# Masked many-head cross-attention: scores by query for the maxima, and a second set by key for the exponentials

## The chip, the cores and the metric

One core of one Trainium2 chip runs the whole program in one launch. The metric is the device time in microseconds (us). The kernel before took 776.32 us (median of three runs, 772.29 to 776.37). The engines are PE (TensorE: matmuls and transposes, with PEld for its weight loads), DVE (VectorE), ACT (ScalarE), POOL (GpSimd) and SP (SyncE, which here issues the DMAs). Each engine works through its own list of instructions in order; semaphores tie the lists together.

## The reference, cut to what matters

A decoder of two layers works on x (16 sequences, 128 tokens, 256 channels). Each of six sublayers normalises x and adds its result: a one-head causal attention, a cross-attention with 16 heads and a boolean mask, a block-sparse feed-forward layer, a 16-head attention, a 16-head windowed attention with another mask, and a mixture of experts. The change is in the second:

```python
qh = (q @ Wq.T + bq).reshape(B, Sq, 16, 16)          # q: normalised x; k, v: ctx
kh = (k @ Wk.T + bk).reshape(B, Sk, 16, 16)
vh = (v @ Wv.T + bv).reshape(B, Sk, 16, 16)
scores = jnp.einsum('bqhd,bkhd->bhqk', qh, kh) / np.sqrt(16)
scores = jnp.where(attention_mask[:, None, :, :], -1e7, scores)
probs = jax.nn.softmax(scores, axis=-1)
out = jnp.einsum('bhqk,bkhd->bqhd', probs, vh)
```

For these inputs no position is masked, but the kernel does not know that and masks by the data.

## The kernel before, in words

The 16 sequences are worked in eight pairs of 256 tokens. A running number U counts pairs through the stages: U 0 to 7 is the one-head attention (stage 0), 8 to 15 the masked many-head stage (stage 1), 16 to 23 the feed-forward layer (stage 2), 24 to 31 the unmasked 16-head attention (stage 3), 32 to 39 the windowed one (stage 4); the experts follow. A loop over U calls `half(U, 0)` and `half(U, 1)` on every engine, one half for each sequence of the pair, and the order in which `half` and its `part0` to `part3` call their steps is the order of the engine's list, written by hand. Steps of pairs U-2 to U+2 lie in one half.

PSUM has eight banks of 128 x 512 numbers in three rings: `pj` (three banks, for projections and transposes), `sc` (four banks, for scores) and `ov` (one bank). A bank's `filled` semaphore counts what PE has put into it, and `drained` what DVE or ACT has taken out; PE waits for `drained` before it writes a bank again. The four heads of a bank make one "group" n, so a half has four groups, one in each `sc` bank.

Stage 1 before. `scores` puts queries on partitions and keys along the free axis. Two of a half's four groups get the mask by a matmul ahead of the scores (`preload`, L462), the two others by a DVE addition (`add_mask`, L1096). DVE takes row maxima (`row_maxima`, L1103), ACT the exponentials, four instructions of 128x128 a group with the maximum as bias (`row_exps`, L1651). The probabilities then have queries on partitions, and the product with the values needs keys there: PE transposes each group (`turn_probs`, L546), and DVE or ACT copies the result out (`copy_probs`, L1110). `probs_times_values` (L558) and `turn_out` (L567) follow, and `norm_heads` (L1133, L1137) divides by the sums.

Stages 3 and 4 do without the transposes. `by_query` (L485) computes scores only for the maxima (`maxima`, L1125). `turn_maxima` (L494) transposes the small table of maxima, ACT copies it out (L1627, mxT), and SP's `shift` (L2102) moves it by DMA into unused rows of the query tile qM, where it works as one more channel against a row of constants in the key tile kM. `by_key` (L514) then computes scores with keys on partitions and the maximum already subtracted, and ACT's `exps` (L1642) takes one 128x512 exponential a group straight from PSUM. `by_query` for a half is issued one half ahead: `following(U, j)` names the half whose maxima are taken while `by_key` of (U, j) is still to come. Both score sets go through the same four `sc` banks in turn.

The blank rows that SP writes to the experts' table (`blank_rows`) lie between the loads of the context in stage 1.

Of the kernel before, what the change touches and what calls it, by code (L numbers as in the profile page):

```python
# [24 lines left out]
P = 128  # L25
F32 = mybir.dt.float32
BF16 = mybir.dt.bfloat16
# [30 lines left out]
for _name, _n in (("bq0", C), ("bk0", C), ("b1", FF), ("bq1", 2 * C), ("bk1", 2 * C), ("gq", C), ("gk", C),  # L58
                  ("gv", C), ("go", C), ("mine", 2), ("unit", 2), ("quarter", 2), ("sixteenth", 2), ("place", B),
                  ("lane", 1)):  # L60
    VEC[_name] = (sum(n for _, n in VEC.values()), _n)
# [10 lines left out]
def program(nc, x, ctxT, ctx, tokq, tokk, mask, ident, causal, causalT, vec, rows, lnb, before, blank,  # L72
# [3 lines left out]
    with stack:  # L76
# [20 lines left out]
        bq = [sb(f"bq{i}", [P, (C, 2 * C)[i]]) for i in range(2)]  # L97
# [18 lines left out]
        def R(name):  # L116
# [23 lines left out]
        kraw = sb("kraw", [P, C, T])  # L140
# [32 lines left out]
        pT = [hT[1][:].rearrange("p a b -> p (a b)")[:, r * 4 * S:(r + 1) * 4 * S].rearrange("p (a s) -> p a s", a=4)  # L173
              for r in range(4)]
        mxg = [mx[0][:, r * 4:(r + 1) * 4] for r in range(4)]
# [68 lines left out]
        def sems(names):  # L244
# [11 lines left out]
        mx_done, ri_done, kM_done, masked_done, s_causT = sems("mx_done ri_done kM_done masked_done s_causT")  # L256
# [10 lines left out]
        spots_done, first_done, one_done, slot_done = sems("spots_done first_done one_done slot_done")  # L267
        den_done, dene_done, deni_done, share_done, comb_done = sems(
            "den_done dene_done deni_done share_done comb_done")
        cnt_done, step_done, many_done, upto_done, reach_done, behind_done, who_done, base_done, row_done, tab_done = sems(  # L270
            "cnt_done step_done many_done upto_done reach_done behind_done who_done base_done row_done tab_done")
# [10 lines left out]
        ACT_TURNS = {1: (2, 6)}  # L282
        DVE_MAXED = {4: (3, 7), 5: (3, 7), 6: ()}
# [23 lines left out]
        def overtaken(U, j):  # L307

            return stage(U) == 1 and (U % PAIRS, j) != (PAIRS - 1, 1)

        def shifted(U):

            return stage(U) in (3, 4)
# [69 lines left out]
        def _(pe):  # L383
# [112 lines left out]
            def by_key(U, j):  # L496

                f, p = U // PAIRS, U % PAIRS
                masks = {3: None, 4: mbT1}[f]
# [8 lines left out]
                pe.wait_ge(s_shift[j], 32 * (att(U) - PAIRS + 1))  # L508
# [10 lines left out]
            def scores(U, j):  # L519

                f, p = U // PAIRS, U % PAIRS
                if j == 0:
                    pe.wait_ge(*emptied("q", U))
                    pe.wait_ge(kM_done, att(U) + 1)
                sides = []
                for n in range(4 * j, 4 * j + 4):
                    b, k = begin("sc", "s", U, n)
                    pe.wait_ge(drained[b], k - 1)
                    added = n not in DVE_MASKED[f]
                    if added:  # L530
                        preload(b, mb0, p, j)
                    sides.append((b, slice(32 * (n % 4), 32 * (n % 4) + 32), added))
                for c in range(C):
                    for b, strip, added in sides:
                        last = mm(bank[b][:, c * T:(c + 1) * T], qT[U % 2][strip, c, j * S:(j + 1) * S],  # L535
                                  kM[U % 2][strip, c, :, j * S:(j + 1) * S], start=not added, stop=True,
                                  skip_group_check=True)
                        if c == C - 1:
                            last.then_inc(filled[b], 1)

            def turn_probs(U, n):
                b, k = begin("pj", "pT", U, n)
# [272 lines left out]
            def half(U, j):  # L815
# [4 lines left out]
                elif f == 1:  # L820
                    scores(U, j)
# [1448 lines left out]
```

## Time and profile before

| what | value |
|---|---|
| median of three runs | 776.32 us |
| the profiled execution | 779.23 us, span 777.4 us |
| PE busy | 742.5 us (96%) |
| DVE busy | 481.2 us (62%) |
| ACT busy | 389.0 us (50%) |
| POOL busy | 297.3 us (38%) |
| mean granted TensorE clock | 0.987 of full |

The profiled execution is one run; its span goes from the first to the last instruction, and its own time is 1.8 us longer. Busy shares are means over stages with different limits, so what a change in one stage is worth has to be read from that stage's stretch: here about 64 to 205 us.

### The profile page before, as it was taken

Reading aid. Unit: us, or ns where it says so; the run is one execution under the profiler, and the core shown is the slowest. Engines: PE = TensorE matmul, PEld = TensorE weight load, DVE = VectorE, ACT = ScalarE, POOL = GpSimd, SP = SyncE. Lnnn points to the kernel's source line nnn. Section 1 sums busy time; section 2 is a strip of 40 time slices with the busy share of each in tenths; the row PEclk is TensorE's granted clock in tenths of the full one; section 3 lists DMA queues with packets and bytes.
Section 4 is the critical chain, followed back from the end, with each engine's and each line's share of the span. In section 5 each row is a group of like instructions: output and inputs, shape, how many; then the busy total and the mean of one; then the engine's idle time right before and its main releaser. Section 6 shows DMA issues by size and latency. Waiting matters only on the chain.

```text
span 777.4 us, 19012 instructions
## 1 busy us (share of the span) xinstructions
PE 742.5 (96%) x7189; PEld 608.0 (78%) x7189; DVE 481.2 (62%) x1388; ACT 389.0 (50%) x951; POOL 297.3 (38%) x397
## 2 busy tenths in 40 slices
PE   8999999999999999999999999999999899899996
PEld 7887777776788888888888887777867667688885
DVE  4686787887654445356555566787856458554435
ACT  3445677777533233436666544444534266266630
POOL 2323333434224213211212255565656435545540
PEclk9999999999999999999999999999989899999999
DMA  8997244300256642101000021000000101245428
GB/s 310 402 220 145 76 109 117 78 15 2 62 139 165 166 128 70 56 2 30 4 3 3 4 90 51 16 16 16 16 30 16 36 31 41 90 138 155 145 87 320
DMA packets 67962, 69.92 MB, mean 90 GB/s; under 512 B 22721, under 2 KB 58561, under 8 KB 66849
## 3 DMA queue, kind: packets, MB, share of 16 engines
q1 hardware_dynamic: 64464, 59.37, 26.5%
q0 software_dynamic: 3408, 9.34, 3.5%
q8 instruction: 59, 0.97, 0.5%
q14 instruction: 31, 0.25, 0.1%
HBM read 39.03 MB, written 29.40 MB: 88 GB/s over the span
## 4 chain that ended last, share of the span: by engine, by line
PE 77%; DVE 10%; ACT 4%; issue 3%; POOL 2%; DMA 2%; SPq 1%; another core or an unknown queue 1%; DVEq 0%; POOLq 0%
PE pj L403 12%; PE pj L396 8%; PE sc L609 7%; PE ov L622 7%; PE ov L558 6%; PE sc L485 4%; PE sc L514 4%; PE pj L390 4%; PE ov L812 4%; PE sc L462 4%; PE sc L804 3%; DVE mx L1103 3%; PE pj L546 2%; PE sc L535 2%; PE pj L567 2%
## 5 line engine op out<-in xcount | busy, mean ns | idle before, releaser
L1642 ACT ACTIVATE pr<-sc 128x512 f32<-128x512 f32 x128 | 66.1, 606 | 72.9 <-PE sc L514 65.6
L1125 DVE TENSOR_REDUCE mx<-sc 128x4 f32<-128x512 f32 x120 | 74.5, 683 | 23.7 <-PE sc L485 21.5
L1651 ACT ACTIVATE pr<-sc,mx 128x128 f32<-128x128 f32 x256 | 72.9, 379 | 31.4 <-DVE mx L1103 30.3
L1883 POOL TENSOR_SCALAR ve<-mv 128x2 f32<-128x2 f32 x40 | 13.3, 333 | 180.6 <-DVE mv L1038 180.2
L609 PE MATMUL sc<-xnT,W 128*128 128x256 f32 x256 | 61.0, 382 | 0.8 <-DVE mx L1125 0.8
L1700 ACT ACTIVATE hT<-sc,vecs 128x256 f32<-128x256 f32 x64 | 30.1, 475 | 62.6 <-PE sc L609 62.6
L622 PE MATMUL ov<-W,hT 128*128 128x256 f32 x256 | 60.1, 379 | 0.0
L1627 ACT ACTIVATE oT<-ov 128x512 f32<-128x512 f32 x48 | 28.9, 602 | 53.9 <-PE ov L558 48.4
L622 PEld LDWEIGHTS ov<-W,hT 128*128 128x128 f32 x256 | 48.5, 190 | 6.7
L1961 POOL DMA_INDIRECT routed_y<-pr,mask x39 | 37.3, 955 | 41.5 <-DVE mask L1379 34.9
L609 PEld LDWEIGHTS sc<-xnT,W 128*128 128x128 f32 x256 | 47.3, 190 | 7.0 <-DVE mx L1125 1.0
L1103 DVE TENSOR_REDUCE mx<-sc 128x4 f32<-128x512 f32 x64 | 42.8, 684 | 13.8 <-PE sc L535 13.8
L1627 ACT ACTIVATE xnT<-pj 128x512 f32<-128x512 f32 (+1 forms) x79 | 38.7, 490 | 18.7 <-PE pj L390 11.3
L1913 POOL TENSOR_TENSOR hT<-hT,rws 128x512 f32<-128x512 f32 x16 | 20.4, 1274 | 63.1 <-DVE hT L1241 63.1
L804 PEld LDWEIGHTS sc<-xnT,cT 128*128 128x128 f32 x312 | 40.5, 191 | 2.5 <-issue 0.7
L546 PE MATMUL pj<-idn,pr 128*128 128x128 f32 x256 | 39.9, 282 | 2.6 <-ACT pr L1651 1.0
L514 PEld LDWEIGHTS sc<-qM,kM 32*128 32x128 f32 x1024 | 32.6, 192 | 12.5 <-issue 12.1
L804 PE MATMUL sc<-xnT,cT 128*128 128x128 f32 x312 | 41.3, 275 | 0.0
L558 PE MATMUL ov<-pr,va 128*32 128x128 f32 x1024 | 38.0, 276 | 3.1 <-issue 2.4
L485 PEld LDWEIGHTS sc<-kM,qM 32*128 32x128 f32 x1024 | 31.5, 186 | 11.0 <-issue 10.0
L546 PEld LDWEIGHTS pj<-idn,pr 128*128 128x128 f32 x256 | 27.6, 141 | 15.2 <-issue 9.5
L1133 DVE RECIPROCAL rin<-pj 128x16 f32<-128x16 f32 x48 | 12.1, 253 | 43.9 <-PE pj L567 36.3
(259 smaller groups left out, 1794.5 us busy)
## 6 DMA issues: line engine op xcount, KB each, us to landing
sorted_x<-more_xT SPq DMA_DIRECT2D x15, 1152.0 KB, 7.9
kM<-sorted_x SPq DMA_DIRECT2D x39, 129.0 KB
cT<-in_ctxT SPq DMA_DIRECT2D x16, 256.0 KB, 3.6
pr<-kept_at SPq DMA_DIRECT2D x32, 128.0 KB, 3.2
W<-in_w SPq DMA_DIRECT2D x2, 1024.0 KB, 13.5
cT<-in_ctx SPq DMA_DIRECT2D x8, 256.0 KB, 3.8
oT<-kept_at SPq DMA_DIRECT2D x16, 128.0 KB, 3.2
hd<-kept_at SPq DMA_DIRECT2D x16, 128.0 KB, 3.3
```

The lines of the kernel that those rows point to most:

```text
L403: last = mm(bank[b][:, j * n:(j + 1) * n], still[:, c, j * S:(j + 1) * S], w[:, c, col:col + n], start=c == 0, stop=c == C - 1)
L514: last = mm(bank[b][:, o:o + S], kM[U % 2][strip, c, i, s], qM[U % 2][strip, c, i, s], start=not added, stop=True, skip_group_check=True)
L546: last = tr(bank[b][:, i * S:(i + 1) * S], pr[n % 4][:, i, :], idn[:])
L558: last = mm(bank[b][32 * i:32 * i + 32, g * S:(g + 1) * S], va[U % 2][:, j, 4 * g + i, :], probs[g][:, i, :], start=True, stop=True, skip_ ...
L609: last = mm(bank[b][:, 0:T], W1[:, d, c * P:(c + 1) * P], xnT[U % 3][:, d, :], start=d == 0, stop=d == C - 1)
L622: last = mm(bank[b][:, j * D:(j + 1) * D], hT[U % 2][:, d, j * S:(j + 1) * S], W2[:, d, :], start=d == 0, stop=d == FF - 1)
L804: last = mm(bank[b][:, i * P:(i + 1) * P], tile_gu[t % 2][:, c, i * EI:(i + 1) * EI], xtT[t % 3][:, c * P:(c + 1) * P], start=c == 0, stop ...
L1103: v.tensor_reduce(mxg[n % 4], four(b), AX.X, ALU.max, negate=True).then_inc(mx_done, 1)
L1125: last = v.tensor_reduce(dst, bank[b][:, :].rearrange("p (c i s) -> p c i s", c=C, i=2), AX.X, ALU.max, negate=True)
L1627: a(dst, src, ACT.Copy, scale=scale).then_inc(drained[b], 1)
L1642: a(pr[n % 4][:], four(b), ACT.Exp).then_inc(drained[b], 1)
L1651: last = a(pr[n % 4][:, i, :], bank[b][:, i * S:(i + 1) * S], ACT.Exp, bias=mxg[n % 4][:, i:i + 1])
```

## The change

Stage 1 takes the form of stages 3 and 4. `scores`, `turn_probs` and their copies go. `by_query` masks all four groups of a half by `preload` with mb0. `by_key` masks nothing: ACT and DVE do it behind it, each for two groups of a half. For the groups 2 and 3, `add_mask` takes the minimum of a score and `hidden` (0 where the key is seen, -1e30 where not); a score less its maximum is never above 0. For the groups 0 and 1, ACT takes Relu of the negated score into SBUF and the exponential in place there, and DVE's `clip` takes the minimum with `seen` (1 or 0). `seen` and `hidden` come from a transposed copy of the mask (`maskT`, 256 KB, a new DMA) and lie in half of the tile that held the copied probabilities; `count_hidden` (four matmuls in all) finds queries that see no key, and `note_seen` lets these see all. `key1` moves half a pair earlier and `value1` likewise; keys are formed by ACT alone (`keys`), not by ACT and POOL. The blank rows of stage 1 are cut into thirds, one after each `shift`.

```diff
             def by_query(U, j):
-                masks = {3: None, 4: mb1}[f]
+                masks = {1: mb0, 3: None, 4: mb1}[f]
...
             def by_key(U, j):
-                masks = {3: None, 4: mbT1}[f]
+                masks = {1: None, 3: None, 4: mbT1}[f]
...
+            def count_hidden(i):
+                b, n = begin("pj", "hidden", i)
+                pe.wait_ge(drained[b], n - 1)
+                mm(bank[b][:, :], onesb[:], seen[:, 4 * i:4 * i + 4, :], start=True, stop=True).then_inc(filled[b], 1)
...
             def probs_times_values(U, j):
-                name, probs = ("s", pr) if shifted(U) else ("pT", pT)
                 for g in range(4):
-                    pe.wait_ge(*emptied(name, U, 4 * j + g))
+                    if U // PAIRS == 1 and g < 2:
+                        pe.wait_ge(clipped, 4 * att(U) + 2 * j + g + 1)
+                    else:
+                        pe.wait_ge(*emptied("s", U, 4 * j + g))
...
             def add_mask(U, n):
+                if U // PAIRS == 1:
+                    v.tensor_tensor(four(b), four(b), over(hidden[:, 2 * p + n // 4, :], 4), ALU.min).then_inc(masked_done, 1)
...
+            def clip(U, n):
+                dve.wait_ge(warmed, 4 * att(U) + 2 * (n // 4) + n % 4 + 1)
+                v.tensor_tensor(pr[n % 4][:], pr[n % 4][:], over(seen[:, 2 * (U % PAIRS) + n // 4, :], 4),
+                                ALU.min).then_inc(clipped, 1)
+            def note_seen(i):
+                b, n = spot["hidden", i]
+                some = seen[:, 4 * i:4 * i + 4, :]
+                dve.wait_ge(filled[b], n)
+                v.scalar_tensor_tensor(some, some, float(S), four(b), ALU.mult, ALU.is_le).then_inc(drained[b], 1)
+                dve.wait_ge(drained[b], n)
+                v.tensor_scalar(hidden[:, 4 * i:4 * i + 4, :], some, 1.0, -NEG, ALU.subtract, ALU.mult)
...
                 if shifted(U):
                     for n in range(4 * j, 4 * j + 4):
                         if n in DVE_MASKED[masking(U)]:
                             add_mask(U, n)
+                if f == 1:
+                    for n in (4 * j, 4 * j + 1):
+                        clip(U, n)
                 if shifted(Z[0]):
                     norm_heads(*Z)
...
+            def below(U, j):
+                for n in (4 * j, 4 * j + 1):
+                    b, k = spot["s", U, n]
+                    act.wait_ge(filled[b], k)
+                    a(pr[n % 4][:], four(b), ACT.Relu, scale=-1.0).then_inc(drained[b], 1)
+                for n in (4 * j + 2, 4 * j + 3):
+                    exps(U, n)
+                for n in (4 * j, 4 * j + 1):
+                    act.wait_ge(*emptied("s", U, n))
+                    a(pr[n % 4][:], pr[n % 4][:], ACT.Exp, scale=-1.0).then_inc(warmed, 1)
```

How the lists move. On PE, the steady pair of stage 1 before (U = 11, from its first half's scores to its second half's last transpose; pj, sc and ov are the rings, L535 is `scores`, L546 `turn_probs`):

```order
L535 MATMUL sc<-kM,qM 128x256 x8
L546 MATMUL pj<-idn,pr 128x128 x4
L396 MATMUL pj<-xnT,Wq 128x256 x4
L558 MATMUL ov<-hT,va 32x128 x16
L546 MATMUL pj<-idn,pr 128x128 x4
L396 MATMUL pj<-cT,Wk 128x256 x4
L546 MATMUL pj<-idn,pr 128x128 x4
L567 MATMUL pj<-idn,oT 128x128 x4
L546 MATMUL pj<-idn,pr 128x128 x4
```

The same engine and place in the changed kernel, both halves of a pair (L457 is `preload`, L480 `by_query`, L534 `probs_times_values`, L509 `by_key`, L489 `turn_maxima`, L543 `turn_out`):

```order
L457 MATMUL sc<-mb,idnb 128x512 x4
L480 MATMUL sc<-kM,qM 128x128 x16
L534 MATMUL ov<-pr,va 32x128 x16
L391 MATMUL pj<-xnT,Wq 128x256 x4
L509 MATMUL sc<-qM,kM 128x128 x16
L489 MATMUL ov<-idn,mx 16x128
L543 MATMUL pj<-idn,oT 128x128 x4
L398 MATMUL pj<-Wv,cT 128x256 x4
L457 MATMUL sc<-mb,idnb 128x512 x4
L480 MATMUL sc<-kM,qM 128x128 x16
L534 MATMUL ov<-pr,va 32x128 x16
L509 MATMUL sc<-qM,kM 128x128 x16
```

The groups of transposes are gone, and between `by_query` and `by_key` stands the product and a projection in the first half, the product alone in the second.

On DVE, one half of stage 1 in the kernel before (L1103 `row_maxima`, L1110 `copy_probs`, L1096 `add_mask`, L1133 and L1137 `norm_heads`):

```order
L1103 TENSOR_REDUCE mx<-sc 128x4
L1110 COPY hT<-pj 128x512
L1103 TENSOR_REDUCE mx<-sc 128x4
L1096 TENSOR_TENSOR sc<-sc,mb 128x512 x2
L1103 TENSOR_REDUCE mx<-sc 128x4 x2
L1110 COPY hT<-pj 128x512 x2
L1133 RECIPROCAL rin<-pj 128x16
L1137 TENSOR_TENSOR hd<-pj,rin 128x256
```

The same place in the changed kernel (L1084 `maxima`, L1052 `add_mask`, L1059 `clip`, L1092 and L1096 `norm_heads`, L1113 `values`, then the next half's `maxima`):

```order
L1084 TENSOR_REDUCE mx<-sc 128x2x2 x4
L1052 TENSOR_TENSOR sc<-sc,hT 128x512 x2
L1059 TENSOR_TENSOR pr<-pr,hT 128x512 x2
L1092 RECIPROCAL rin<-pj 128x16
L1096 TENSOR_TENSOR hd<-pj,rin 128x256
L1113 TENSOR_TENSOR va<-pj,rws 128x32x16
L1084 TENSOR_REDUCE mx<-sc 128x2x2 x4
```

The copies are gone; two clips stand behind the masked minima and ahead of the next half's four reductions.

## Rows read from the trace of the kernel before

**Rows 1.** Busy time by engine: a pair of stage 1, one of stage 3.

```profile
119.50:136.47 16.97, 16.42 (x169) 12.40 (x169) 13.77 (x28) 12.67 (x40) 6.78 (x9) 1.00 0.33 87
372.12:388.03 15.91, 15.91 (x247) 13.15 (x243) 9.28 (x21) 10.29 (x22) 3.38 (x4) 1.00 0.01 4
```

**Rows 2.** PE in time (start, us, what): masks of pair 8, pair 15, stage 2's begin.

```profile
63.55 0.59 PE L462 MATMUL sc<-mb,idnb 128*128 128x512 bf16 x2
...
185.66 1.15 PE L535 MATMUL sc<-kM,qM 32*128 32x256 f32 x16
...
204.96 1.99 PE L609 MATMUL sc<-xnT,W 128*128 128x256 f32 x8
```

**Rows 3.** PE in time: half a pair of stage 3.

```profile
382.44 1.17 PE L514 MATMUL sc<-qM,kM 32*128 32x128 f32 x32
383.54 0.28 PE L494 MATMUL ov<-idn,mx 128*16 128x128 f32 x1
383.65 0.60 PE L567 MATMUL pj<-idn,oT 128*128 128x128 f32 x4
384.09 1.89 PE L396 MATMUL pj<-xnT,Wqkv 128*128 128x256 f32 x8
385.91 1.17 PE L485 MATMUL sc<-kM,qM 32*128 32x128 f32 x32
387.02 1.08 PE L558 MATMUL ov<-pr,va 128*32 128x128 f32 x32
388.03 1.99 PE L396 MATMUL pj<-xnT,Wqkv 128*128 128x256 f32 x8
389.95 1.17 PE L514 MATMUL sc<-qM,kM 32*128 32x128 f32 x32
```

**Rows 4.** The chain that ended last, in stage 4 (start, us, what): four mask matmuls.

```profile
570.16 0.86 PE sc L462 x4
```

**Rows 5.** DVE in time, in stage 3.

```profile
384.92 0.74 DVE L1032 BATCH_NORM_STATS2 bst<-X 128x6 f32<-128x256 f32 x2
385.70 0.25 DVE L1038 BATCH_NORM_AGGREGATE mv<-bst 128x2 f32<-128x6 f32 x2
387.10 2.49 DVE L1125 TENSOR_REDUCE mx<-sc 128x4 f32<-128x512 f32 x4 [1.15 <-PE sc L485]
391.81 0.26 DVE L1133 RECIPROCAL rin<-pj 128x16 f32<-128x16 f32 x1 [2.22 <-PE pj L567]
392.10 0.42 DVE L1137 TENSOR_TENSOR hd<-pj,rin 128x256 f32<-128x256 f32 x1
```

**Rows 6.** ACT in time, in stage 3.

```profile
390.06 1.93 ACT L1676 ACTIVATE qM<-pj,bq,vecs 128x256 f32<-128x256 f32 x4 [1.30 <-PE pj L396]
391.87 2.07 ACT L1642 ACTIVATE pr<-sc 128x512 f32<-128x512 f32 x4
393.78 0.25 ACT L1627 ACTIVATE mxT<-ov 16x128 f32<-16x128 f32 x1
```

**Rows 7.** DVE groups by line (count, busy us, mean ns): two sources in SBUF; mask additions.

```profile
L1206 DVE TENSOR_TENSOR hT<-hT,pr 128x512 f32<-128x512 f32 x16 | 11.5, 764 | 10.2 <-DMA pr<-kept_at 10.2
L1206 DVE TENSOR_TENSOR hT<-hT,hd 128x512 f32<-128x512 f32 x8 | 5.1, 684 | 0.0
L1096 DVE TENSOR_TENSOR sc<-sc,mb 128x512 f32<-128x512 f32 x32 | 20.6, 690 | 0.0
```

**Rows 8.** ACT in time, in stage 2: a Relu.

```profile
209.62 0.48 ACT L1700 ACTIVATE hT<-sc,vecs 128x256 f32<-128x256 f32 x1 [0.39 <-PE sc L609]
```

**Rows 9.** Windows around two falls of the clock (length, PE, PEld, DVE, ACT, POOL, PEclk).

```profile
600.90:604.60 3.70, 1.95 (x16) 0.66 (x13) 1.84 (x4) 0.00 (x0) 3.25 (x4) 0.94 0.31 109
604.60:611.00 6.40, 6.40 (x53) 4.76 (x51) 0.82 (x3) 2.04 (x4) 0.85 (x2) 0.50 0.01 1
645.40:648.70 3.30, 3.30 (x15) 2.82 (x15) 2.11 (x9) 0.18 (x1) 1.58 (x4) 0.52 0.00 0
```

**Rows 10.** DMA issues (KB each, median us from issue to landing).

```profile
kept_at<-mask SPq DMA_DIRECT2D x8, 16.0 KB, 1.5
```

More of the change, by code:

```diff
@@ L69, with program @@
 NROW = sum(n for _, n in ROWS.values())
-def program(nc, x, ctxT, ctx, tokq, tokk, mask, ident, causal, causalT, vec, rows, lnb, before, blank,
+def program(nc, x, ctxT, ctx, tokq, tokk, mask, maskT, ident, causal, causalT, vec, rows, lnb, before, blank,
             w_qk, w_ov, w_q0, w_k0, w_v0, w_r0, w_1, w_2, w_qkv, w_o1, w_x, w_g, w_gu,
@@ L96, in program @@
         mbT1 = sb("mbT1", [P, B, S], BF16)
-        bq = [sb(f"bq{i}", [P, (C, 2 * C)[i]]) for i in range(2)]
+        bq = [sb(f"bq{i}", [P, 2 * C]) for i in range(2)]
         mhalf = sb("mhalf", [P, 4])
@@ L517, in by_key @@
                                 last.then_inc(filled[b], 1)
[L519 to L542, printed above, removed]
-                pe.wait_ge(drained[b], k - 1)
-                pe.wait_ge(*emptied("s", U, n))
-                for i in range(4):
-                    last = tr(bank[b][:, i * S:(i + 1) * S], pr[n % 4][:, i, :], idn[:])
-                last.then_inc(filled[b], 1)
+            def count_hidden(i):
+                b, n = begin("pj", "hidden", i)
+                pe.wait_ge(drained[b], n - 1)
+                if i == 0:
+                    pe.wait_ge(s_seen, 1)
+                    pe.wait_ge(s_counts, 1)
+                mm(bank[b][:, :], onesb[:], seen[:, 4 * i:4 * i + 4, :], start=True, stop=True).then_inc(filled[b], 1)
             def probs_times_values(U, j):
@@ L879, in part1 @@
                 if f == 1:
[L880 removed]
+                    value1(U + 1)
                 elif f == 3:
@@ L1900, in x_norm @@
                 last.then_inc(xn_done, 1)
-            def masked_keys(W):
-                pool.wait_ge(*emptied("k", W))
-                for o in range(C):
-                    for i in two:
-                        last = g.tensor_scalar(kM[W % 2][:, o, i, :], kraw[:, o, :], V("bk0", o), V("mine", i), ALU.add, ALU.mult)
-                last.then_inc(kM_done, 1)
             def rotate(W, i):
@@ L2092, in _ @@
                 blank_rows(i)
-            for p in range(2, PAIRS):
-                sp.wait_ge(*full("v", PAIRS + p - 2))
-                sp.dma_start(cT[p % 2][:], ctxT[:, :, p * T:(p + 1) * T]).then_inc(s_ct[p % 2], 16)
-                blank_rows(p + 3)
             def shift(U, j):
@@ L2103, in shift @@
                                  mxT[j][8 * i:8 * i + 8, :]).then_inc(s_shift[j], 16)
+            for U in range(PAIRS - 1, 2 * PAIRS):
+                for j in two:
+                    N = following(U, j)
+                    if stage(N[0]) == 1:
+                        shift(*N)
+                    p = U + 3 - PAIRS
+                    if j == 0 and 2 <= p < PAIRS:
+                        sp.wait_ge(*full("v", PAIRS + p - 2))
+                        sp.dma_start(cT[p % 2][:], ctxT[:, :, p * T:(p + 1) * T]).then_inc(s_ct[p % 2], 16)
+                    at = 2 * (U - PAIRS + 1) + j
+                    if at < 16:
+                        blank_rows(15 + at, BINS // P // 45)
+            for at in (16, 17):
+                blank_rows(15 + at, BINS // P // 45)
             def spread(U):
```

232 lines of the change are left out of this document (61 added, 171 removed).

## The prediction

> **What bounds the kernel now.** I read the windows by stage first, then PE in order of time, then the other engines' rows for the prices. In stage 1 a pair takes 16.97 us, and PE is busy 16.42 of them at the full clock; DVE has 13.77, ACT 12.67 [rows 1]. So the order of PE's list sets the time there, and DVE, at 81%, is not far behind. Stage 3 has the form that stage 1 is to take, without masks: 15.91 us, all of them PE, with DVE at 9.28 [rows 1]. The reader is to see two things: the new form can be PE's alone, and it is so where DVE has little to do. Stage 1 reaches from the masks of pair 8 at 63.55 (its first scores: masks and 0.52 later, 64.07) over the scores of pair 15 at 185.66 to stage 2's first up-projection at 204.96 [rows 2]. Seven pairs between pair 8 and 15 take 121.6, the tail behind pair 15's first scores 19.3. Stage 2 begins with PE's list at once, so I carry what stage 1 gains or loses to the end unchanged. The profiled execution took 779.23 us, 2.9 more than the median of 776.32; the sum is made in the profile's times, and its difference is put on the median.
>
> **PE's own work.** A half of stage 3 gives the prices as start to start [rows 3]: scores by key 1.10, turning the maxima 0.11, turning the output 0.44, a projection 1.82 (1.92 behind the product), the product 1.01; four mask matmuls 0.86 [rows 4]. In the new list the first half has masks 0.86, scores by query 1.10, product 1.01, projection 1.92, scores by key 1.10, 0.11, 0.44 and a projection 1.82: 8.36. The second half has one projection and one group of four transposes (0.44): 6.88. The pair is 15.2 us of PE against 16.42: 1.2 us less work, and 1.7 less than the pair's time.
>
> **The chain that I expect to bind.** Both sets of scores go through the same four banks. So the scores by key must be read out by ACT before the next half's scores by query are written, and those must be reduced by DVE before the next scores by key are. DVE goes in order: the reductions that release PE stand behind two masked minima, two clips, the norm of the heads and, in the first half, the forming of the values, in the second, the statistics. A clip waits for ACT's exponential in place, which ACT does behind two Relus and two exponentials. Priced from the start of one set by key to the next:
> - scores by key 1.17 [rows 3]; then ACT may be still busy with the queries of the next pair (1.93 [rows 6]) and start up to 0.45 late in the first half.
> - two Relus and two exponentials from PSUM. Four exponentials took 2.07, with the next instruction 1.91 after the first's start [rows 6], a Relu of half the columns 0.48 [rows 8]; bounds for a whole Relu 0.48 and 0.96 (twice that row), taken 0.49, since the exponential of 512 columns is the nearest in size: 1.95. The masked minima, 0.64 each (20.6 over 32, [rows 7]), lie beside the Relus.
> - the first exponential in place, SBUF to SBUF, which no row shows; bounds 0.25 (the 128-column copy, [rows 6]) and 0.96 (that Relu doubled); taken as the exponential of 512, with the hand-over to DVE 0.61.
> - two clips. No row has this form; two sources in SBUF of this size took 11.5/16 = 0.72 and 5.1/8 = 0.64 each [rows 7]. Bounds 0.32 (half of it, one source being repeated over heads) and 0.76 (the row's mean); taken 0.64: 1.28. The second in-place exponential lies beside the first clip.
> - the norm 0.29 + 0.42 = 0.71 [rows 5]; in the first half the values, 0.64 by the row of the same size that reads a bank [rows 7]; in the second the statistics 0.78 + 0.25 = 1.03 [rows 5].
> - four reductions 2.49 [rows 5].
>
> First half 1.17 + 1.95 + 0.61 + 1.28 + 0.71 + 0.64 + 2.49 = 8.85, up to 9.30 with ACT late; second half 9.24. The pair is 18.1 to 18.5 long; I take 18.1, because neighbours on an engine overlap by some hundredths. That is 2.9 more than PE's own work, so PE waits. In the second half only the product (1.01) stands between scores by query and by key, and the reductions take 2.49: there a gap of 1.5 to 2.8 us opens in every pair even where all else goes well. Behind PE's waiting scores by key are queued both turns and a projection, and for these wait SP's shift, DVE's norm and ACT. The least a pair can take is 15.2 + 1.6 = 16.8.
>
> **The shift.** SP moves the turned maxima by two DMAs. A mask load lands 1.5 us after its issue [rows 10]; two in a row lie between 1.5 and 3.0, taken 2.8. In the steady pair they start half a period ahead and have about 4 us to spare: nothing. The load of the transposed mask and its issue are early, cost nothing while they land ahead of pair 8, and would cost their delay otherwise.
>
> **Head, middle, tail.** Ahead of pair 8's scores by key nothing covers the first reductions: masks and scores by query 1.96, reductions 2.6 with their hand-over, turn 0.1, the key projection 1.8, the count 0.2, second scores by query 1.96, reductions 2.6, in all 11.2, so 63.55 + 11.2 = 74.8, against 64.07. Seven pairs: 7 × 18.1 = 126.7. Three of the four `note_seen` fall within these, two DVE instructions each (0 if they fit a gap, 1.4 by [rows 7]; taken 1.0): 3.0. Stage 0's last residual additions, 0.72 in each of two pairs [rows 7]: 1.4. Pair 15's first scores by key are at 74.8 + 131.1 = 205.9. The tail has no next half: 1.17, six ACT instructions 2.92, the copy of the maxima 0.2 and the shift 2.8, now uncovered, are 7.1; then scores by key to the first exponential in place 3.73, clip and hand-over 0.72, the product 1.4 with its start: 5.9. Stage 2 begins at 218.9, against 204.96: +13.9, or 790.2 on the median. The shorter tail (13.0 for 19.3) is the one gain. That keys are formed by ACT alone adds 1.93 per pair to ACT, behind its six instructions in the second half; the reductions run meanwhile, and it costs nothing unless ACT is late for the next Relu.
>
> **The clock.** Before, stage 1 had no gap that mattered and 1.00. In stage 4, after 3.70 us with PE busy for 1.95, the granted clock was 0.50 (the lower level, 1.2 GHz) for 6.40 us, and a second time 0.52 for 3.30 [rows 9]. With a gap of up to 2.8 us per pair, some pairs will see it. At the lower level PE's share of a half takes up to twice as long, but half of that fills the gap it came from: a fall of 3.3 us costs the chain about 1.0, one of 6.4 about 2.5. I take three falls at 1.5: +4.5, and predict 795.
>
> The Trainium skill, "TensorE: Matmul & The Clock Gate", section "Loop structure matters more than you think", says that VectorE emptying PSUM between groups of matmuls doesn't cost the clock, and that a long wait for a DMA does. By that rule the reductions' gaps leave it full and the time is 790; the fall above came after a stretch in which PE was still fed in pieces, and it speaks against the rule. No stretch of before shows a single gap of this length in a dense list.
>
> **Rivals.**
> - The chain binds and the clock holds: 790. For it: PE is busy for 84% of each pair. Against it: [rows 9].
> - The clock falls at every gap: 7 × 2.5 = 17.5 on 790, so 808. For it: the gaps are alike, so what happens in one pair happens in all. This is the dearest of the clock's cases.
> - DVE and ACT run ahead and PE never waits for the reductions, as in stage 3: seven pairs at 15.2 give -12.4, the head +10.7, the tail -6.3: -8, so 768, faster than before. For it: stage 3's 15.91 with PE busy throughout. Against it: DVE had 9.28 there, and has 5.1 more here (two minima, two clips per half). It decides if a half's chain falls below 7.6.
> - The chain fits but the one gap stays: 16.8 a pair, -1.2 in seven, +10.7, -6.3, minus or plus what `note_seen` costs: 778, no change. It needs clips and in-place exponentials at their lower bounds.
> - The shift is late in every half (6 us instead of 2.8, with other queues' traffic): 813.
>
> **How the numbers follow.** Forecast with some falls of the clock 0.36; clock holds 0.24; falls everywhere 0.22; no change 0.08; faster 0.05; late shift 0.05. The range for 8 in 10 is 783 to 811: the chain's pair at 17.2 (all unknown prices low) to 18.5 with every gap cooled. A measurement of this kernel tells about 0.5% from no change, 772.4 to 780.2. Faster 0.05, same 0.08, slower 0.87.
>
> **What would show it.** In the window of a middle pair: a period near 18.1, PE busy near 15.2 of it at the full clock, a gap ahead of the second scores by key that the reductions end. On DVE the first clip waits for ACT, and no reduction waits for PE. Stage 2's first up-projection near 219 to 223, and stages 2 to 4 as long as before. A granted clock under 1.00 in stage 1 decides between the first three cases. I am wrong if the pair is under 17 us, if the reductions wait for PE (then PE bounds), if clips take under 0.4 us, or if the scores by key wait for the shift.

## The result, and the profile after

| | before | changed |
|---|---|---|
| median of four runs, same chip | 774.31 us | 817.45 us |
| ratio | | 1.058 (95%: 1.0537 to 1.0623) |
| profiled execution, span | 779.23, 777.4 us | 817.23, 815.4 us |
| scores by query / by key of pair 8 | 64.07 | 82.26 |
| the same of pair 15 | 185.66 | 232.98 |
| first up-projection of stage 2 | 204.96 | 250.61 |

The change makes the kernel 5.8% slower. The side was forecast, the size was not: 795 (range 783 to 811) against 817.45. The loss lies in stage 1, which ends 45.7 us later: 18.2 of that come before pair 8's first scores by key, 29.1 in the seven pairs, and the tail behind them is 1.7 shorter. After stage 1 the changed execution is 7.6 us shorter than the profiled one of before, so that 38.0 are left; the medians are 43.1 apart. 5.3 us of the 7.6 fall in stage 4 (565.74 to 614.76 in before, 612.27 to 656.01 here). Before had two stretches there with a granted clock of 0.74 and 0.79, the second around the fall of [rows 9]; in the changed execution they have 1.00 and 0.88.

The windows of the changed kernel, whose columns are those of [rows 1]: the seven pairs, the tail, and then pair 12 in its two halves, from one set of scores by key to the next.

```profile
82.26:232.98 150.72, 121.30 (x1680) 93.14 (x1684) 93.46 (x186) 81.45 (x172) 31.55 (x35) 0.93 0.17 48
232.98:250.61 17.63, 12.88 (x155) 9.46 (x156) 11.22 (x29) 8.07 (x17) 5.92 (x7) 0.79 0.29 63
...
171.28:181.06 9.78, 6.76 (x114) 5.02 (x114) 6.17 (x11) 5.61 (x12) 1.27 (x2) 1.00 0.20 60
181.06:191.50 10.44, 10.44 (x126) 8.29 (x126) 6.58 (x14) 6.30 (x13) 2.94 (x4) 0.84 0.19 50
```

Seven pairs take 150.7 us where 131.1 were forecast and before had 121.6; PE waits for 29.4 of them, and the clock is 0.93. The two halves are bound by different things. In the first one PE is busy for 6.76 of 9.78 at the full clock; in the second it never waits, for 10.44 at 0.84. That 0.84 is a mean: from 182.50 to 184.50 the clock is 0.50 (the lower of its two levels, 1.2 GHz), from 185.50 on it is 1.00. PE of this pair in order of time shows why; the rows to compare are [rows 2, 3]:

```profile
171.28 1.17 PE L509 MATMUL sc<-qM,kM 32*128 32x128 f32 x32
...
176.75 1.28 PE L534 MATMUL ov<-pr,va 128*32 128x128 f32 x32
181.06 1.69 PE L509 MATMUL sc<-qM,kM 32*128 32x128 f32 x32 [3.03 <-DVE mx L1084]
182.68 0.38 PE L489 MATMUL ov<-idn,mx 128*16 128x128 f32 x1
182.85 1.06 PE L543 MATMUL pj<-idn,oT 128*128 128x128 f32 x4
183.71 2.52 PE L391 MATMUL pj<-cT,Wk 128*128 128x256 f32 x8
186.06 0.60 PE L385 MATMUL pj<-idn,xw 128*128 128x128 f32 x4
```

The scores by key of the second half wait 3.03 us for DVE's reductions, and the work right behind the wait runs slowly: the transposes take 1.06 and the key projection 2.52, where [rows 3] has 0.60 and 1.89. What DVE and ACT did meanwhile (DVE first, to be compared with [rows 5], then ACT, with [rows 6]):

```profile
172.56 1.30 DVE L1052 TENSOR_TENSOR sc<-sc,hT 128x512 f32<-128x512 f32 x2 [1.64 <-PE sc L509]
175.83 1.29 DVE L1059 TENSOR_TENSOR pr<-pr,hT 128x512 f32<-128x512 f32 x2 [1.97 <-ACT pr L1583]
177.04 0.25 DVE L1092 RECIPROCAL rin<-pj 128x16 f32<-128x16 f32 x1
177.39 0.42 DVE L1096 TENSOR_TENSOR hd<-pj,rin 128x256 f32<-128x256 f32 x1
177.74 0.68 DVE L1113 TENSOR_TENSOR va<-pj,rws 128x512 f32<-128x512 f32 x1
178.33 2.48 DVE L1084 TENSOR_REDUCE mx<-sc 128x4 f32<-128x512 f32 x4
```

```profile
171.39 1.93 ACT L1591 ACTIVATE qM<-pj,bq,vecs 128x256 f32<-128x256 f32 x4 [1.30 <-PE pj L391]
173.21 1.10 ACT L1578 ACTIVATE pr<-sc 128x512 f32<-128x512 f32 x2
174.16 1.12 ACT L1571 ACTIVATE pr<-sc 128x512 f32<-128x512 f32 x2
175.12 1.20 ACT L1583 ACTIVATE pr<-pr 128x512 f32<-128x512 f32 x2
```

This is the chain that the prediction priced, link by link. The reader is to see that DVE has no idle time from the first clip at 175.83 to the end of the reductions, and that it waits 1.97 for the exponential in place (L1583) and 1.64 for the scores.

The head (PE, to the first of [rows 2]):

```profile
63.16 1.03 PE L457 MATMUL sc<-mb,idnb 128*128 128x512 bf16 x4
64.12 1.17 PE L480 MATMUL sc<-kM,qM 32*128 32x128 f32 x32
67.99 0.27 PE L489 MATMUL ov<-idn,mx 128*16 128x128 f32 x1 [2.70 <-DVE mx L1084]
68.21 1.40 PE L445 MATMUL pj<-pT,xw 128*128 128x128 f32 x8
69.40 3.34 PE L391 MATMUL pj<-cT,Wk 128*128 128x256 f32 x8
75.26 0.70 PE L385 MATMUL pj<-idn,xw 128*128 128x128 f32 x4 [2.51 <-ACT cnT L1556]
75.75 1.91 PE L457 MATMUL sc<-mb,idnb 128*128 128x512 bf16 x4
77.59 1.90 PE L480 MATMUL sc<-kM,qM 32*128 32x128 f32 x32
79.42 1.99 PE L391 MATMUL pj<-xnT,Wq 128*128 128x256 f32 x8
```

The tail (PE; pair 15's two sets of scores by key are at 232.98 and 242.00):

```profile
238.52 1.54 PE L534 MATMUL ov<-pr,va 128*32 128x128 f32 x32 [2.29 <-DVE pr L1059]
240.00 2.08 PE L640 MATMUL pj<-Wx,lnbs 128*128 128x256 f32 x4
242.00 1.62 PE L509 MATMUL sc<-qM,kM 32*128 32x128 f32 x32
...
248.33 0.44 PE L576 MATMUL pj<-idn,nm 128*128 128x128 f32 x2 [2.38 <-DVE hd L1096]
```

PE waits here for the clips and then for the norm of the heads. The last scores by key follow PE's own projection without a wait, so it is not the shift that holds them.

### The profile page after: what moved, and what is told of

It reads as the page before. It is cut to its first block, busy times and chain, and to the rows that moved or that the text cites. A ratio compares the mean times of both kernels' runs of the same rounds, so it can differ in the third digit from the quotient of the medians.

```text
span 815.4 us, 19980 instructions
## 1 busy us (share of the span) xinstructions
PE 747.5 (92%) x7749; PEld 613.8 (75%) x7753; DVE 480.6 (59%) x1381; ACT 383.5 (47%) x831; POOL 281.2 (34%) x365
## 3 DMA queue, kind: packets, MB, share of 16 engines
q0 software_dynamic: 3408, 9.34, 3.1%
## 4 chain that ended last, share of the span: by engine, by line
PE 70%; DVE 10%; ACT 9%; issue 4%; DMA 2%; POOL 2%; SPq 1%; another core or an unknown queue 1%; DVEq 0%; POOLq 0%
PE pj L398 11%; PE pj L391 7%; PE sc L585 7%; PE ov L598 7%; PE sc L509 6%; PE sc L480 6%; PE ov L534 5%; PE pj L385 4%; PE sc L457 4%; PE sc L780 3%; ACT pr L1571 3%; DVE mx L1084 3%; PE ov L788 2%; DVE pr L1059 2%; PE pj L543 2%
## 5 line engine op out<-in xcount | busy, mean ns | idle before, releaser
L1084 DVE TENSOR_REDUCE mx<-sc 128x4 f32<-128x512 f32 x184 | 114.2, 683 | 36.4 <-PE sc L480 35.0
L1571 ACT ACTIVATE pr<-sc 128x512 f32<-128x512 f32 x160 | 84.0, 608 | 68.3 <-PE sc L509 61.0
L509 PE MATMUL sc<-qM,kM 32*128 32x128 f32 x1536 | 60.5, 297 | 21.9 <-DVE mx L1084 21.9
L509 PEld LDWEIGHTS sc<-qM,kM 32*128 32x128 f32 x1536 | 51.0, 198 | 38.8 <-issue 38.4
L480 PEld LDWEIGHTS sc<-kM,qM 32*128 32x128 f32 x1536 | 48.7, 191 | 17.4 <-issue 16.4
L534 PE MATMUL ov<-pr,va 128*32 128x128 f32 x1536 | 56.5, 278 | 4.6 <-DVE pr L1059 2.3
L480 PE MATMUL sc<-kM,qM 32*128 32x128 f32 x1536 | 57.9, 288 | 0.8 <-ACT pr L1571 0.6
L534 PEld LDWEIGHTS ov<-pr,va 128*32 128x32 f32 x1536 | 39.2, 110 | 14.5 <-issue 3.5
L1591 ACT ACTIVATE qM<-pj,bq,vecs 128x256 f32<-128x256 f32 x64 | 30.9, 564 | 32.3 <-PE pj L391 32.3
L1591 ACT ACTIVATE kM<-pj,vecs 128x256 f32<-128x256 f32 x64 | 30.9, 562 | 16.9 <-PE pj L391 16.8
```

What stands on the lines that cost most here:

```text
L480: last = mm(bank[b][:, o:o + S], qM[U % 2][strip, c, i, s], kM[U % 2][strip, c, i, s], start=not added, stop=True, skip_group_check=True)
L509: last = mm(bank[b][:, o:o + S], kM[U % 2][strip, c, i, s], qM[U % 2][strip, c, i, s], start=not added, stop=True, skip_group_check=True)
L534: last = mm(bank[b][32 * i:32 * i + 32, g * S:(g + 1) * S], va[U % 2][:, j, 4 * g + i, :], pr[g][:, i, :], start=True, stop=True, skip_gro ...
L1084: last = v.tensor_reduce(dst, bank[b][:, :].rearrange("p (c i s) -> p c i s", c=C, i=2), AX.X, ALU.max, negate=True)
L1571: a(pr[n % 4][:], four(b), ACT.Exp).then_inc(drained[b], 1)
L1591: last = a(dst[:, c, i, :], bank[b][:, c * T:(c + 1) * T], ACT.Identity, bias=shift[:, 2 * c + i:2 * c + i + 1], scale=V(scale, i))
```

## The experiments

Theory 1 of the first runs is that first halves are bound by the chain through ACT and DVE and second halves by PE's list at a lowered clock; the later expectations each say what theirs is. "Pairs" is the time from pair 8's first scores by key to pair 15's (150.7 us in the changed kernel), "tail" from there to stage 2 (17.6), both from the windows of each profile; halves and waits too come from one profiled execution of each kernel. Kernels that ran on different chips are compared by their ratio to the kernel before.

**1. No clips.**
```diff
-                if f == 1:
-                    for n in (4 * j, 4 * j + 1):
-                        clip(U, n)
```


> Leaves out the two clips of each half of stage 1 (masked keys of groups 0 and 1 keep weight); the product waits for the exponentials in place instead. Theory 1 (first half of a pair bound by the chain through ACT and DVE, second half by PE's own list at a clock that the gap has lowered): on DVE 1.21 us of clips and 0.7 us of waiting for the exponentials go in each half, the first half falls from 9.78 to about 7.9 us and the gap ahead of the second scores by key from 3.03 to about 1.1; the second half falls only by what the clock gives back, up to 1.4 us. Seven pairs: 13 to 23 us, the tail 1 to 2, so 793 to 803 us. Rival (the clips lie beside a wait for PE, which takes their place): within 4 us of the changed kernel, 813 to 821 us.

790.04 us, ratio 1.020 (1.012 to 1.029), below the range of theory 1. Its first halves are 8.30 us, 0.4 more than expected, and its second ones 8.8 to 9.0, mostly PE's list at the full clock; one, pair 12's, is 10.43 at 0.84.

```profile
81.50:211.45 129.95, 113.64 (x1681) 89.19 (x1684) 76.71 (x158) 81.04 (x173) 32.34 (x35) 0.97 0.19 55
211.45:224.86 13.41, 10.75 (x156) 8.32 (x156) 7.90 (x25) 7.85 (x17) 4.85 (x6) 0.87 0.38 86
```

Pairs fall by 20.8, the tail by 4.2. The clips are on the path, and with them goes part of the gap by which PE cooled: the wait ahead of the second scores by key is 1.75 instead of 3.03.

**2. The gap filled with idle work.**
```diff
+                if f == 1 and j == 1:
+                    k, names = turns["pj"], RINGS["pj"]
+                    spare = names[k % len(names)]
+                    pe.wait_ge(drained[spare], k // len(names))
+                    for i in range(8 if p < 2 else 12):
+                        mm(bank[spare][:, :], idnb[:], mb0[:, 0:4, :], start=True, stop=True)
```


> Adds idle work: ahead of each second scores by key of stage 1, 12 matmuls of 128x512 (8 in the first two pairs) into a bank that is free there, 2.6 us (1.7) in the gap of 3.03 us (1.75). Theory 1: the clock stays at 1.00 in the second halves, these fall from 10.2-10.4 us to 8.8-9.2 where no count of hidden keys stands, the first halves stay at 9.8: seven times 1.0 to 1.5, so 806 to 811 us. Rival (the lower clock comes from something else, or costs nothing since PE has time): unchanged at 815 to 819 us, or slower by the added matmuls. A second rival (the clock makes nearly all of the loss against the forecast): 795 us or less.

817.8 us, ratio 1.057 (1.050 to 1.064): no gain, as the first rival has it. But the halves show something else. Where no count of hidden keys stands (pairs 10, 12), the second half fell from 10.44 to 9.34, as theory 1 said: that is the clock's price there, 1.1 us. The first half right behind such a second half fell too, from 9.78 to 9.41 and 9.25. Where a count stands (9, 11, 13) it is 12.9 to 13.3, which was 11.3 to 13.3. PE of pair 11 in that kernel:

```profile
156.47 1.17 PE L515 MATMUL sc<-qM,kM 32*128 32x128 f32 x32 [0.18 <-issue]
...
158.12 1.89 PE L391 MATMUL pj<-cT,Wk 128*128 128x256 f32 x8
162.30 0.66 PE L385 MATMUL pj<-idn,xw 128*128 128x128 f32 x4 [2.28 <-DVE hd L1102]
162.79 1.70 PE L457 MATMUL sc<-mb,idnb 128*128 128x512 bf16 x4
164.42 2.09 PE L480 MATMUL sc<-kM,qM 32*128 32x128 f32 x32
```

The key projection is back at 1.89, and then the next x's transposes wait 2.28 for the norm of the heads. Behind that wait the clock is down (0.59 from 162.30 to 166.50), and the scores by query take 2.09. So the idle work held the clock up in pairs 10 and 12 only. The ring pj has three banks; with the count as one more user the transposes get the bank of `turn_out`, which DVE empties behind the clips. Of the changed kernel's own wait there, the slow projection had covered most (0.62 of wait was left in this pair). And the last half, in which PE had no wait ahead of the scores by key, became 2.0 longer by the added matmuls.

**3. No count.**
```diff
-                if U in (PAIRS - 1, PAIRS + 1, PAIRS + 3, PAIRS + 5):
-                    count_hidden((U - PAIRS + 1) // 2)
```


> Leaves out the count of hidden keys and the rule for queries that see none: four matmuls on PE and eight DVE instructions go, and no bank of the ring is used for them. Theory 1: second halves with a count lose the wait of turning x for the norm of the heads (0.6 to 0.9 us) and the 1.0 us of DVE, about 1.1 us each in three pairs; in the head the ring still makes PE wait for the copy of stage 0's context, or 2.5 us go. So 3 to 8 us less: 809 to 814 us. Rival (DVE's 1.0 us lies hidden and the ring moves the wait to another bank): 815 to 819 us.

809.34 us, ratio 1.044 (1.038 to 1.051): pairs 142.3, 8.4 less, and 2.0 less in the head. So the count, that the sum had at 0.2 on PE and 1.0 on DVE, costs a few us more than these. Part of it is the clock: pairs 10 and 12 of this one execution, neither with a count, differ by it. PE from pair 10's second scores by key to pair 12's first:

```profile
133.79 1.17 PE L509 MATMUL sc<-qM,kM 32*128 32x128 f32 x32 [2.65 <-DVE mx L1082]
...
135.45 1.89 PE L391 MATMUL pj<-cT,Wk 128*128 128x256 f32 x8
...
143.14 1.17 PE L509 MATMUL sc<-qM,kM 32*128 32x128 f32 x32 [0.46 <-DVE mx L1082]
...
152.38 1.17 PE L509 MATMUL sc<-qM,kM 32*128 32x128 f32 x32 [2.72 <-DVE mx L1082]
...
154.51 3.08 PE L391 MATMUL pj<-cT,Wk 128*128 128x256 f32 x8
...
162.86 1.17 PE L509 MATMUL sc<-qM,kM 32*128 32x128 f32 x32
```

Pair 10 has the full clock in both halves and takes 9.17 + 9.35 = 18.52; pair 12 (9.78 + 10.49 = 20.27) has 0.84 in its second half. The first halves differ as well. Where the clock held, PE waits 0.46 between the query projection and the scores by key, and ACT uses that time to form the queries: pair 11's first Relu starts 0.22 behind its scores, and its first half is 9.24. In pair 11's second half the clock fell, PE ends last and has no such wait, and pair 12's first Relu starts 0.75 behind its scores.

**4. Masks of the second scores on PE.**
```diff
-                masks = {1: None, 3: None, 4: mbT1}[f]
+                masks = {1: hidden, 3: None, 4: mbT1}[f]
```
(and plain exponentials, without minima and clips)

> The scores by key are masked on PE, by four matmuls that add the tile of hidden keys ahead of them, as stage 4 does; Relu, exponential in place, minima and clips go, ACT takes four plain exponentials from PSUM. PE has 2 x 0.86 us more per pair, DVE 5 us less. Theory 1: the chain of the first half falls to 1.17 + 0.8 + 2.0 + norm, values and maxima 3.8, about 7.8 us, below PE's 7.9; the pair is PE's list alone, 16.9 to 17.3 us at the full clock instead of 20.8, seven pairs 25 to 27 us less, tail 2 to 3 less: 786 to 792 us. Rival (PE's second half was the bound and gets 0.86 longer; the clock stays low): 812 to 822 us.

792.62 us, ratio 1.024 (1.017 to 1.031): just above the range. Pairs 129.8 at clock 1.00, tail 11.4.

```profile
81.37:211.16 129.79, 126.20 (x1737) 91.35 (x1740) 59.95 (x131) 67.21 (x144) 32.52 (x35) 1.00 0.20 56
```

PE waits for 3.6 of these 129.8. Its second halves are 9.7 to 9.9 (8.8 + 0.86), PE's list alone; the first ones 8.39, above the 7.8 expected. PE's added masks cost less than the clips did.

**5. Queries late on ACT.**
```diff
                 if shifted(N[0]):
                     copy_out(mxT[N[1]][:], "mT", *N)
+                if f == 1 and j == 0 and stage(U + 1) == 1:
+                    queries(U + 1)
```


> Moves the forming of the next pair's queries on ACT in stage 1 behind the half's six Relus and exponentials and the copy of the maxima; nothing else. Theory 1: in the changed kernel ACT starts the first Relu of a pair's first half 0.75 us late because of it (152.10 where the scores by key ended at 151.35), and all of the chain behind it moves: the first half falls from 9.78 to about 9.0 us in the steady pairs, the second stays: 4 to 7 us less, 810 to 813 us. Rival (the queries come late for the next scores by query, or the copy of the outputs behind them makes PE wait): 815 us or more.

822.55 us, ratio 1.062 (1.057 to 1.067): theory 1 was wrong here. From pair 10 on the first halves became 11.2 to 12.8, since PE's next scores by query need these queries:

```profile
153.75 1.04 PE L457 MATMUL sc<-mb,idnb 128*128 128x512 bf16 x4 [2.72 <-ACT qM L1591]
```

The 0.75 us by which ACT comes late can't be had by moving the queries behind. The second halves without a count are 9.34 at the full clock here.

**6. Counts in stage 0.**
```diff
-                if U in (PAIRS - 1, PAIRS + 1, PAIRS + 3, PAIRS + 5):
-                    count_hidden((U - PAIRS + 1) // 2)
+                if U in range(PAIRS - 4, PAIRS):
+                    count_hidden(U - PAIRS + 4)
```
(and the same for `note_seen`; the mask's copy that both need moves to an earlier pair)

> The four counts of hidden keys and what DVE makes of them move into the last four pairs of stage 0; stage 1 has none. With nothing left out, it takes away the slot in the ring of three banks by which the next x's transposes wait for the norm of the heads. Theory 1 (the ring's slot is a cost, of 1.0 to 1.5 us in three pairs and some in the head): as the run without counts, whose time was 8 us below the changed kernel's: 806 to 813 us. Rival (stage 0, where PE is as busy, pays as much): 814 to 819 us.

815.45 us, ratio 1.053 (1.047 to 1.058), not told apart from the changed kernel. Pairs fell to 141.9, as without counts, but pair 8's first scores by key came at 89.19 instead of 82.26: stage 0 paid 6.9 of the 8.8.

**7 and 8. A first reordering, and the same with masks on PE for two groups.** The edits of runs 5 and 6 in one kernel, with the key projection ahead of the second scores by key on PE and DVE's norm, values and statistics behind the next reductions (the edits of runs 11 and 12, from pair 8 on); run 8 has also
```diff
-                masks = {1: None, 3: None, 4: mbT1}[f]
+                masks = {1: hidden, 3: None, 4: mbT1}[f]
```
with the minima of groups 2 and 3 left on DVE.

> The same work in another order: counts in stage 0, queries on ACT behind the half's exponentials, the next key projection on PE ahead of the second scores by key (into the gap), and on DVE the norm of the heads, the values and the statistics behind the next half's reductions, where DVE waited 1.5 us for the scores by key. Theory 1 (the order of three lists is what costs, not the added operations): the chain of a half is 1.15 + 1.95 + 0.7 + 1.2 + 2.5 + 0.3 = 7.8 us, PE has 8.2 in the first half and 7.0 in the second: 16.0 to 16.4 a pair instead of 20.3, with the clock up: 776 to 786 us. Rival (clips and minima make the chain long in any order): 795 us or more.

> As the reordered one, and groups 0 and 1 of a half are masked on PE by two matmuls of the tile of hidden keys ahead of the scores by key, instead of Relu, exponential in place and clip; groups 2 and 3 keep the minima on DVE. PE has 0.43 us more per half, the chain loses 0.7 + 1.2. Theory 1: PE's list binds: 8.6 and 7.4, with the loop over the four banks at 7.3 to 8.0: 16.1 to 16.7 a pair, and the tail behind pair 15's first scores falls from 17 to about 12 us: 772 to 780 us, level with the kernel before. Rival (PE's added masks and the head cost as much as the clips): 785 us or more.

834.38 us, ratio 1.077 (1.072 to 1.082), and 817.02 us, ratio 1.056 (1.049 to 1.062): far from the forecasts, by two mistakes of mine. The first was the late queries again (waits of 2.76). The second was that stage 0's last residual additions moved with the values, while the product waits for their bank (pair 8 in run 7):

```profile
99.02 1.94 PE L534 MATMUL ov<-pr,va 128*32 128x128 f32 x32 [4.00 <-DVE X L1044]
```

Pair 8 and the first half of pair 9 took 15 to 18 us a half. In run 7 the second halves behind them were 8.76, which spoke for trying the order again.

**9 and 10. The reordering without these.** The edits of runs 11 and 12 (below), and, on PE and in the same way on ACT (run 10 has besides, as run 8, the masks of groups 0 and 1 on PE):
```diff
+                if f == 1 and j == 0 and stage(U + 1) == 1:
+                    query1(U + 1)
                 if attends(Z[0]):
                     probs_times_values(*Z)
```

> The same work in another order, without the two mistakes that the slow run of the first reordering showed (queries came late for the next scores by query; stage 0's last residuals held a bank). From pair 9 or 10 on: the key projection fills the gap ahead of the second scores by key; on DVE norm, values and statistics stand behind the next reductions, in the time in which DVE waited for the scores by key; the query projection and its copy go ahead of the product; the count goes to a first half, where no transposes wait behind it. Theory 1 (order, not the added operations, makes most of the loss in the steady pairs): chain of a half 7.8 us, PE 8.2 and 7.0, pair 16.0 to 16.6 instead of 20.3 to 21.1 from pair 10 on, clock near 1.00 there: seven pairs 124 to 129 us instead of 150.7, so 790 to 797 us. Rival (clips and minima make the chain long in any order; a pair stays above 18): 803 us or more.

> That reordered kernel, with groups 0 and 1 of each half masked on PE by two matmuls of the tile of hidden keys, in place of Relu, exponential in place and clip. Theory 1: PE has 0.43 us more per half and binds at 8.6 and 7.4, the chain loses 1.9: 16.1 to 16.8 a pair, and the tail behind pair 15's first scores by key falls from 17.6 to 13 or 14 us, pairs 8 and 9 lose 1 to 2 us a half: 780 to 789 us. Rival (the pair is bound by the loop over the four banks, and PE's masks lie on it): 795 us or more.

806.56 us, ratio 1.050 (1.045 to 1.055), a miss: by its time and its pair of 20.3 us the rival's side, though not for the rival's reason. And 789.1 us, ratio 1.026 (1.021 to 1.031), 0.1 above theory 1's range. In run 9 a new wait took the place of the old one: the query projection, put ahead of the product, needs x's copy, which stands on ACT behind the keys.

```profile
162.28 3.64 PE L391 MATMUL pj<-xnT,Wq 128*128 128x256 f32 x8 [2.05 <-ACT xnT L1577]
```

First halves were 8.9 and second ones 11.4, with the projection at 3.64 behind the wait. With masks on PE (run 10) ACT has no exponentials in place ahead of that copy, the wait is 1.02, and the second halves are 9.27 at clock 1.00.

**11. Key projection in the gap, count in the first half.**
```diff
             def part2(U):
+                if U > PAIRS and stage(U + 2) == 1:
+                    key1(U + 2)
...
                     value1(U + 1)
+                if U in (PAIRS + 1, PAIRS + 3, PAIRS + 5):
+                    count_hidden((U - PAIRS + 1) // 2)
```


> The changed kernel with two edits of that order alone: the key projection ahead of the second scores by key from pair 9 on, and the count in the first half. DVE's and ACT's orders stay. Theory 1: the projection fills the gap, so that the clock stays up, and PE's second half falls to 7.0 us, but the chain through ACT and DVE keeps first halves at 9.8 (10.7 with a count) and takes the second ones at 9.2: 19.0 to 19.9 a pair instead of 20.3 to 21.1; 7 to 12 us less, 806 to 811 us. Rival (PE's order is enough): 798 us or less; second rival (nothing is gained, the wait moves): 814 us or more.

802.37 us, ratio 1.044 (1.038 to 1.049): 0.014 under the changed kernel's ratio. In the steady pairs the halves are 9.17 and 9.35 (10.15 for a first half with a count). Theory 1 kept first halves at 9.8, which was wrong: the clock is up, PE waits 0.54 ahead of their scores by key, and ACT is less late, as in run 3. So the time lies below its range.

```profile
81.06:220.35 139.29, 116.21 (x1683) 87.30 (x1684) 92.96 (x186) 80.11 (x172) 31.57 (x35) 0.99 0.18 52
```

**12. And DVE's norm, values and statistics late.**
```diff
+                if f == 1 and U > PAIRS + 1 and (U, j) != (2 * PAIRS - 1, 1):
...
+                            behind_maxima.append(lambda: norm_heads(*Z))
+                    behind_maxima.append(lambda: (part1, part3)[j](U))
+                    behind_maxima.append(lambda: (alone0, alone1)[j](U))
+                    return
```
The next half empties the list behind its reductions.

> The kernel with the key projection in the gap and the count in the first half (802.4 us), and on top of it, from pair 10 on, the norm of the heads, the values and the statistics on DVE behind the next half's reductions instead of ahead of them; the query projection stays behind the product. Theory 1 (DVE's order is on the chain): first halves 1.1 + 0.75 for ACT's queries + 1.95 + 0.7 + 1.2 + 2.5 + 0.3 = 8.5 instead of 9.17, second ones bound by ACT's copy of x and the query projection at 8.8 to 9.0 instead of 9.35: about 1 us a pair in five or six pairs, 795 to 798 us. Rival (the time moves to the wait for x's copy, as in the first half's mistake before: 11.4): 803 us or more; second rival (DVE's order is not on the chain): 800 to 803 us.

795.05 us, ratio 1.035 (1.032 to 1.039), as theory 1 said. First halves are 8.4 to 8.6 (9.2 with a count), second ones 8.7 to 8.8.

```profile
83.14:214.55 131.41, 116.86 (x1683) 86.85 (x1684) 91.41 (x179) 80.42 (x173) 29.22 (x31) 0.99 0.19 55
```

The seven pairs take 131.4, against 150.7, with all the work that the change adds. No run beat the kernel before.

## Why the prediction was wrong

**Right.** Stage 1 carries the loss and hands it to the end. The chain through ACT and DVE binds first halves; its prices hold: two clips 1.21 (177.04 less 175.83; forecast 1.28), two Relus and two exponentials 1.91 (1.95), the exponential in place to the clip 0.71 (0.61), norm and values 1.29 (1.35), reductions 2.48 (2.49). Run 1 shows that the clips lie on it. A whole pair came out near its price where the clock held and no count stood: 18.52 in run 3, for 18.1 to 18.5. In the steady pairs it is the reductions, not the shift, that end the wait of the scores by key.

**The step that failed** is "The pair is 18.1 to 18.5 long", as the length of every pair, and with it the clock's term, "three falls at 1.5". Measured were 20.1 to 21.4 from pair 10 to pair 14, and 150.7 for seven pairs against 131.1. That makes 19.6 of the 31.7 us by which stage 2 begins later than the sum's 218.9 (which left 4.5 for the clock to be added); the head makes 7.5 and the tail 4.6. Seven pairs of 18.52 would take 129.6: pairs 10 to 14 lost 10.4 against that and pairs 8 and 9 lost 10.7. The parts, some of which overlap:

- *ACT comes late.* I allowed 0 to 0.45 and took 0. In pair 12 the scores by key end at 172.45 and the first Relu starts at 173.21: 0.76. With 0.2 of hand-overs the first half is 9.78, not 8.85. Run 3 shows that 0.5 of this is the clock's doing.
- *The second half is PE's own.* I added up PE's list per half as the program writes it, 8.36 and 6.88, and set the chain beside these. From one set of scores by key to the next, the way the chain was priced, PE has 6.4 and then 8.8: 1.10 + 0.11 + 0.44 + 1.82 + 0.44 + 0.86 + 1.10 + 1.01 + 1.92. The total is the same, so the sum did not show it. But 8.8 of PE against a chain of 9.24 leaves 0.4 for anything that slows PE.
- *The clock.* "half of that fills the gap it came from" was wrong: PE cools in the first half's gap and pays in the second half, where it is the bound. The granted clock is 0.83 to 0.85 in the second halves of all five pairs from 10 to 14. One such fall costs 1.1 in that half and 0.5 in the next first half, by ACT; run 3's two pairs differ by 1.75. Five at that price would be at most some 8.7 of the 10.4, an estimate. The case in which the clock falls at every gap was nearest, though it priced a fall at 2.5. Run 2 gained nothing in all because behind a count another wait took the gap's place, and the clock fell there.
- *The ring.* "The count 0.2" left out that it takes a slot among three banks. Runs 2 and 3 show the wait and its price; in the steady pairs of run 11, where no transposes wait behind the count, there is neither it nor the low clock.
- *Pairs 8 and 9* have halves of 11.2 to 13.3, where stage 0's last residuals, contexts and transposes stand between. I had 1.4 for these; together they are 47.7, which is 7.3 more than two pairs like the 12th.
- *The head.* 19.1 us from the masks of pair 8, not 11.2: stage 0's last context (1.2) and x's transposes (0.5) were left out, PE then waits 2.51 for a bank of the ring behind the context's copy, and the projection, masks and scores at 3.34, 1.91 and 1.90 are 3 us longer than at the full clock.
- *The tail*, 17.6 for 13.0, has a clock of 0.79 on a path that was priced at 1.00. From scores by key to scores by key it takes 9.0 for 7.1; the shift, priced into that, does not end it, PE's product behind the clips does. From there to stage 2 it takes 8.6 for 5.9: transposes that wait 2.38 for the norm stand ahead of the last product, and the sum did not have them. How much of the 4.6 is the clock was not measured.

The rule of the Trainium skill that was weighed ("TensorE: Matmul & The Clock Gate", section "Loop structure matters more than you think": VectorE emptying PSUM does not cost the clock) is told there of a loop whose next matmuls follow at once. This list is not such a loop: no DMA ends the wait of 3.03 us, DVE's reductions do, and 0.84 follows. So the use that the prediction weighed, a full clock and 790, is not borne out.

So the cost of the pairs is one of order more than of operations. Runs 11 and 12 keep every operation and take 19.3 of the 29.1 us that the pairs had lost; runs 1, 4 and 10, which leave out or replace the clips, get about as far. What no run took away is the head: every one of them has pair 8's first scores by key at 80 to 89 us, where before had its scores at 64, and in run 12 the head is 19.1 of the 26.6 us by which stage 2 still begins late. That filling the head would bring the new form level with the old one was not tried.

## What to carry to other kernels

Where two products take turns in the same banks, price the loop from one fill to the same fill of the next half on every engine, the matmul list included, and not by the program's sections: equal totals hide which half has no slack. A small instruction that begins a bank of a short ring moves every later user by one, so look up whose release each of them then waits for. On an in-order engine, put what nobody waits for into the wait that is there anyway, but first list who needs it next: late queries, late residuals and an early projection each made a new wait of 2 to 4 us. And a slowed stretch may be paid for twice: here the low clock lengthened one half and also took away the short wait in which ACT got ready for the next.

## What the runs showed of the hardware

A wait that ends a stretch of PE does not always cost the clock, and its length alone does not decide. After 3.03 us the half behind it had 0.84 (pair 12), and after 2.28 us the next 4.2 had 0.59 (run 2, pair 11). But after 2.72 us in run 5 the masks and scores took 1.04 and 1.17, the prices of the full clock. Within one execution both happened: in run 3 it was 1.00 after 2.65 and 0.84 after 2.72; in run 1 it was 1.00 after 1.78 (pair 11) and 0.84 after 1.75 (pair 12); in run 6 it was 1.00 after 3.03 (pair 11) and 0.84 after 2.72 (pair 10). In runs 10 and 11, whose longest waits in the steady pairs were 1.0 and 1.5 us, the seven pairs ran at 1.00 and 0.99. What decides between these was not settled.

An in-place exponential of 512 columns in SBUF took 0.52 from start to start of the next (two in 1.04, 175.12 to 176.16), and a minimum of two f32 sources in SBUF, one of them repeated over four heads, 0.60 (two in 1.21).
